# The linear memory's denominators in one bank, its main part divided one token tile at a time

## What is computed

```python
q = x @ Wq.T; k = x @ Wk.T; v = x @ Wv.T          # x normalised; 512, 128 and 128 columns
qh = q.reshape(b, s, N_QUERY, N_HEAD, D_HEAD)     # 4 x 8 heads of 16 columns
scores = jnp.einsum('bsqhd,bthd->bqhst', qh, kh) * scale
probs = jax.nn.softmax(scores, axis=-1)
a_dot = jnp.einsum('bqhst,bthd->bsqhd', probs, vh)
sigma_q = jax.nn.elu(q.reshape(b, s, N_QUERY, D_KV))
a_mem = sigma_q @ memory / (sigma_q @ memory_norm)   # memory 128 x 128, memory_norm 128 x 1
w = jax.nn.sigmoid(memory_weight)
out = a_dot * (1.0 - w) + a_mem * w
```

## Time and profile before

| | us |
|---|---|
| median of three runs (5053.01 to 5055.21) | 5054.02 |
| the profiled execution | 5102.55 |
| its span, first to last instruction | 5100.8 |
| PE busy in the span | 4587.9 (90%) |
| DVE busy | 3619.3 (71%) |
| ACT busy | 2408.7 (47%) |
| POOL busy | 716.7 (14%) |

### The profile page before, as it was taken

One profiled execution on the slowest core, in us unless ns is written; L12 is line 12 of the kernel. 1 busy time (PEld: TensorE's weight loads), 2 busy tenths in 40 slices (PEclk: granted clock), 3 DMA queues, 4 the chain that ended last, 5 costly groups with the idle time before them and its releaser, 6 DMA issues.

```text
span 5100.8 us, 144724 instructions
## 1 busy us (share of the span) xinstructions
PE 4587.9 (90%) x63104; PEld 3208.2 (63%) x63104; DVE 3619.3 (71%) x7890; ACT 2408.7 (47%) x4592; POOL 716.7 (14%) x909
## 2 busy tenths in 40 slices
PE   5799999999999998499999999999999999999988
PEld 4677777777777776456546646645654654665564
DVE  3666776666667666276787788778778778867876
ACT  3233433333333333164564565466456457546645
POOL 0000000000000000112211211221221221122121
PEclk9899999999999998699999999999999999999999
DMA  2222222222222222100000000000000000000000
GB/s 61 48 62 67 68 71 64 61 61 61 61 62 61 61 66 68 65 1 18 1 18 17 10 9 18 18 1 18 17 1 18 17 10 10 18 18 1 18 9 9
DMA packets 352134, 171.76 MB, mean 34 GB/s; under 512 B 300016, under 2 KB 300784, under 8 KB 350736
## 3 DMA queue, kind: packets, MB, share of 16 engines
q1 hardware_dynamic: 342528, 145.20, 10.7%
q10 hardware_dynamic: 8976, 17.30, 1.2%
HBM read 93.74 MB, written 67.63 MB: 32 GB/s over the span
## 4 chain that ended last, share of the span: by engine, by line
PE 43%; DVE 10%; ACT 3%; issue 1%; POOL 1%; DMA 1%; SPq 0%; DVEq 0%; ACTq 0%; POOLq 0%
PE row_psum L1698 9%; PE row_psum L1673 9%; PE row_psum L40 5%; DVE smax L1951 5%; PE row_psum L42 5%; PE row_psum L41 5%; PE row_psum L1686 4%; PE row_psum L1742 2%; ACT xr_hi L1325 1%; PE row_psum L1726 1%; PE row_psum L1463 1%; DVE probs L1931 1%; DVE stats L1785 1%; POOL rstd L1268 1%; PE row_psum L1645 1%
## 5 line engine op out<-in xcount | busy, mean ns | idle before, releaser
L1951 DVE TENSOR_REDUCE smax<-row_psum 128x1 f32<-128x512 f32 x2048 | 1269.3, 681 | 90.7 <-PE row_psum L1673 89.2
L1398 ACT ACTIVATE probs<-row_psum 128x512 f32<-128x512 f32 x2048 | 1092.6, 601 | 364.8 <-PE row_psum L1686 345.2
L1673 PE MATMUL row_psum<-k_stack,q_stack 64*128 64x512 f32 (+1 forms) x2048 | 738.0, 437 | 50.6 <-DVE smax L1951 24.5
L1686 PE MATMUL row_psum<-q_stack,k_stack 64*128 64x512 f32 (+1 forms) x2048 | 730.8, 457 | 20.8 <-ACT probs L1398 8.2
L1673 PEld LDWEIGHTS row_psum<-k_stack,q_stack 64*128 64x128 f32 (+1 forms) x2048 | 350.5, 186 | 504.0 <-DVE smax L1951 374.0
L1698 PE MATMUL row_psum<-probs,v_aug 128*32 128x512 f32 x4096 | 539.6, 604 | 1.7 <-ACT av_sb L1414 0.4
L1686 PEld LDWEIGHTS row_psum<-q_stack,k_stack 64*128 64x128 f32 (+1 forms) x2048 | 318.3, 184 | 220.2 <-ACT probs L1398 152.5
L868 DVE TENSOR_TENSOR lane_t<-lane_t,lane_p 128x30 f32<-128x30 f32 (+14 forms) x960 | 318.3, 332 | 33.0
L865 DVE TENSOR_TENSOR lane_p<-lane_t 128x30 f32<-128x30 f32 (+14 forms) x960 | 315.6, 329 | 23.5
L40 PE MATMUL span_bank<-x_hi,w_hi 128*128 128x256 f32 x1024 | 301.6, 295 | 33.6 <-DVE x_lo L841 33.0
L40 PE MATMUL row_psum<-wf_hi,xr_hi 128*128 128x320 f32 (+1 forms) x1024 | 331.1, 323 | 0.5 <-DVE xr_lo L1819 0.3
(11 more groups left out here) (209 smaller groups left out, 9883.8 us busy)
## 6 DMA issues: line engine op xcount, KB each, us to landing
x_sp<-in_x ACTq DMA_DIRECT2D x33, 512.0 KB, 4.1
tri_dram<-tri SPq DMA_DIRECT2D x256, 64.0 KB, 2.0
lane_t<-tri_dram SPq DMA_DIRECT2D x32, 512.0 KB, 4.7
inv_dram<-lane_t SPq DMA_DIRECT2D x32, 512.0 KB, 2.6
inv_b<-inv_dram SPq DMA_DIRECT2D x256, 64.0 KB, 2.3
x_res<-in_x SPq DMA_DIRECT2D x32, 512.0 KB, 3.9
x<-x_res SPq DMA_DIRECT2D x32, 512.0 KB, 3.8
xs<-x SPq DMA_DIRECT2D x16, 1024.0 KB, 5.5
```

The costliest lines, as they stand in the source:

```text
L1398: act.activation(probs[:, h % PROBS, tt, :], ps[:, m % STACK_BANKS, :], ACT.Exp, scale=float(DH) ** -0.5).then_inc(exp_ready, 1)
L1673: pe.matmul(ps[:, bank, :], q_stack[rows, qt, P * st:P * st + P], k_stack[rows, kv, :], start=True, stop=True).then_inc(max_mm, 1)
L1686: pe.matmul(ps[:, m % STACK_BANKS, :], k_stack[rows, kv, P * tt:P * tt + P], q_stack[rows, qt, :], start=True, stop=True).then_inc(score_m ...
L1951: dve.tensor_reduce(smax[:, g, st:st + 1], ps[:, bank_of("max", NT * g + st), :], AX.X, ALU.max).then_inc(max_ready, 1)
```

## The change

Each 129-column product is split. The denominators come first: `memory_norms(n)` multiplies, for group n, the four token tiles of `q_elu` with the norm column alone, four matmuls with one moving column each, into sixteen neighbouring columns of bank 7. It stands at four places of PE's loop (`NORM_SLOTS`): in both halves of step 3 and in the first halves of steps 4 and 5. DVE takes one reciprocal and one scaling of all sixteen in step 5. The main part keeps 128 columns; the four results of a token tile fill one bank, 6 or 7 in turn, and DVE multiplies them in one instruction of 512 columns. `MEM_LAG` is 6 in place of 5, so tiles 0 to 3 come in steps 6 to 9, and bank 7 joins the ring at step 10 in place of 9. Tile t waits for `amem_ready` of tile t-2 in place of t-1, and tile 1 for the reciprocals, which have to be out of bank 7. The first group of denominators also waits for the last `q_lo`, since bank 7 holds group 3 of q until DVE has taken that.

```diff
--- before.py
+++ after.py
@@ -1016,10 +1016,12 @@
 TURN_LAG = AV_LAG + 4
 OUT_LAG = TURN_LAG + 1
 MAXT_LAG = 4
-MEM_LAG = 5
+MEM_LAG = 6
+NORM_SLOTS = ((3, 0), (3, 1), (4, 0), (5, 0))
 STACK_BANKS = 3
 RING = (3, 4, 5)
 RING_LAST = 7
+MEM_BANKS = (6, 7)
 PROBS = 7
 NORM_STEP = NH + 1
 LEFT_STEPS = (NH + 3, NH + 5, NH + 6, NH + 11)
@@ -1133,7 +1135,7 @@
         k_mm = sem("row_k_mm"); khi_ready = sem("row_khi"); klo_ready = sem("row_klo"); v_mm = sem("row_v_mm"); vT_ready = sem("vT_ready")
         vtok_mm = sem("vtok_mm"); v_ready = sem("row_v_ready")
         ksel_mm = sem("ksel_mm"); keven_ready = sem("keven_ready"); kodd_ready = sem("kodd_ready"); qsel_mm = sem("qsel_mm"); qstack_ready = sem("qstack_ready")
-        mem_mm = sem("mem_mm"); amem_ready = sem("amem_ready"); amem_added = sem("amem_added")
+        mem_norm_mm = sem("mem_norm_mm"); mem_rc_ready = sem("mem_rc_ready"); mem_mm = sem("mem_mm"); amem_ready = sem("amem_ready"); amem_added = sem("amem_added")
         max_mm = sem("max_mm"); max_ready = sem("max_ready"); maxT_mm = sem("maxT_mm"); shift_ready = sem("shift_ready"); shift_in = sem("shift_in")
         score_mm = sem("score_mm"); exp_ready = sem("exp_ready"); av_mm = sem("av_mm"); av_ready = sem("av_ready")
         avT_mm = sem("avT_mm"); avn_ready = sem("avn_ready"); adot_added = sem("adot_added"); dve_own = sem("row_dve_own")
@@ -1633,17 +1635,25 @@
 
             def attention(b, following):
 
+                def memory_norms(n):
+
+                    pe.wait_ge(qelu_ready, at(b, NQ, n + 1))
+                    if n == 0:
+                        pe.wait_ge(qlo_ready, at(b, NQ, NQ))
+                    for t in range(NT):
+                        last = pe.matmul(ps[:, RING_LAST, NQ * t + n:NQ * t + n + 1], q_elu[:, n, P * t:P * t + P],
+                                         mem_aug[:, DKV:DKV + 1], start=True, stop=True)
+                    last.then_inc(mem_norm_mm, 1)
+
                 def memory(t):
 
-                    if t == 0:
-                        pe.wait_ge(qelu_ready, at(b, NQ, NQ))
-                        pe.wait_ge(qlo_ready, at(b, NQ, NQ))
-                    else:
-                        pe.wait_ge(amem_ready, at(b, NT, t))
+                    if t == 1:
+                        pe.wait_ge(mem_rc_ready, at(b, 1, 1))
+                    if t >= 2:
+                        pe.wait_ge(amem_ready, at(b, NT, t - 1))
                     for n in range(NQ):
-                        c0 = (DKV + 1) * (n % 2)
-                        last = pe.matmul(ps[:, 6 + n // 2, c0:c0 + DKV + 1], q_elu[:, n, P * t:P * t + P],
-                                         mem_aug[:, :], start=True, stop=True)
+                        last = pe.matmul(ps[:, MEM_BANKS[t % 2], DKV * n:DKV * n + DKV], q_elu[:, n, P * t:P * t + P],
+                                         mem_aug[:, 0:DKV], start=True, stop=True)
                     last.then_inc(mem_mm, 1)
 
                 def ring_bank(kind, n):
@@ -1732,6 +1742,8 @@
                             maximum(g, 2 * j + 1)
                         if g < NH and now:
                             score(*now[1])
+                        if (g, j) in NORM_SLOTS:
+                            memory_norms(NORM_SLOTS.index((g, j)))
                         if j == 0 and 0 <= g - MEM_LAG < NT:
                             memory(g - MEM_LAG)
                     quad, i = divmod(g - 3 - TURN_LAG, 4)
@@ -1919,19 +1931,21 @@
                 elu_exp(b, 2)
                 take_q_lo(1)
 
+                def memory_reciprocals():
+                    dve.wait_ge(mem_norm_mm, at(b, NQ, NQ))
+                    rc = mem_rc[:, :, :].rearrange("p t n -> p (t n)")
+                    mark(dve.reciprocal(rc, ps[:, RING_LAST, 0:NT * NQ]))
+                    dve.wait_ge(dve_own, own[0])
+                    dve.tensor_scalar(rc, rc, mem_w[:, 0:1], None, ALU.mult).then_inc(mem_rc_ready, 1)
+
                 def memory(t):
                     dve.wait_ge(mem_mm, at(b, NT, t + 1))
-                    pv = ps[:, 6:8, 0:2 * (DKV + 1)].rearrange("p c (n e) -> p c n e", n=2)
-                    rc = mem_rc[:, t, :].rearrange("p (c n) -> p c n", c=2)
-                    mark(dve.reciprocal(rc, pv[:, :, :, DKV]))
-                    dve.wait_ge(dve_own, own[0])
-                    mark(dve.tensor_scalar(rc, rc, mem_w[:, 0:1], None, ALU.mult))
-                    dve.wait_ge(dve_own, own[0])
-                    for c in range(2):
-                        last = dve.tensor_tensor(a_mem[:, t, 2 * DKV * c:2 * DKV * c + 2 * DKV].rearrange("p (n e) -> p n e", n=2),
-                                                 pv[:, c, :, 0:DKV],
-                                                 rc[:, c, :].rearrange("p (n o) -> p n o", o=1).to_broadcast([P, 2, DKV]), ALU.mult)
-                    last.then_inc(amem_ready, 1)
+                    if t == 0:
+                        dve.wait_ge(mem_rc_ready, at(b, 1, 1))
+                    dve.tensor_tensor(a_mem[:, t, :].rearrange("p (n e) -> p n e", n=NQ),
+                                      ps[:, MEM_BANKS[t % 2], :].rearrange("p (n e) -> p n e", n=NQ),
+                                      mem_rc[:, t, :].rearrange("p (n o) -> p n o", o=1).to_broadcast([P, NQ, DKV]),
+                                      ALU.mult).then_inc(amem_ready, 1)
 
                 for g in range(NH + OUT_LAG):
                     quad, i = divmod(g - 3 - OUT_LAG, 4)
@@ -1949,6 +1963,8 @@
                         if g < NH:
                             dve.wait_ge(max_mm, at(b, NT * NH, NT * g + st + 1))
                             dve.tensor_reduce(smax[:, g, st:st + 1], ps[:, bank_of("max", NT * g + st), :], AX.X, ALU.max).then_inc(max_ready, 1)
+                        if (g, st) == (NORM_SLOTS[-1][0], 2):
+                            memory_reciprocals()
                         if st == 2 and 0 <= g - MEM_LAG < NT:
                             memory(g - MEM_LAG)
                     if g in (1, 2):
```

## The result

The changed kernel takes 5174.49 us (median of four runs, 5168.76 to 5182.03) against 5054.61 for the kernel before on the same chip (four runs, 5053.01 to 5063.09). The ratio is 1.0223, 95% interval 1.0197 to 1.0248: 2.2% slower, 119.9 us between the medians, where 5070 us had been forecast.

What follows compares the result with a forecast made beforehand. DVE looked like the bound in the memory stretch, PE afterwards. DVE's 1.74 us saving a batch was outweighed by PE's slots and waits: values about 1.0 us late, 16 us in 16 batches, on 5054.02: 5070 us (5060 to 5082).

Steps and rivals of the forecast that it cites:

- r14: DVE's reduction number 14, counted as 4 × step + tile; forecast to start 0.50 us late, at 82.53 instead of 82.03.
- DVE's saving: Memory tiles and reciprocals on DVE: four tiles save 2.20 us, new reciprocal and scaling cost 0.46, net 1.74 a batch.
- A slot's price: PE time of four one-column denominator matmuls, eight passes: 0.81 us plus 0.09 for the slower instruction behind, 0.90 in all.
- Rival 3: Weight loads hidden on PE, so a slot costs nothing: 16 - 38 = -22 us, 5032; chance 0.09.
- rival 4: Weight loads unhidden on PE, so a slot costs 1.5 us: +39 us, 5109; chance 0.09.
- Steps 3 to 5 and the `q_lo` wait: PE becomes the bound: first slot waits for the fourth q_lo, DVE idles between reductions, reduction 22 starts 1.79 us late.
- Step 9: Bank 7 joins the ring later, so DVE gets a new idle of 0.79 us before reduction 38.
- the chain: Reduction 32, transposes, matmuls, exp, then ACT's shift ending at 100.5, for which maximum product 37 must wait.
- Rival 1: No stall at step 9: shift in time or product 38 clear of it; -2 us, 5052; chance 0.22.
- Who takes it on: From step 11 PE is the bound; values start about 1.0 us late in each batch, 16 us in 16.
- The clock: TensorE's granted clock, read as 1.00 (2.4 GHz) in the stretch; a reading below 1.00 would show the forecast wrong.
- Rival 2: DVE alone counts and PE's waits absorb the slots: -28 us, 5026; chance 0.10.

## Where the prediction held and where it failed

At full clock the working can be read against the changed kernel's own fourth batch. Times are from that batch's first reduction; the reductions are numbered as in the prediction.

| | before | forecast | full clock | third batch |
|---|---|---|---|---|
| r14 | 9.91 | 10.41 | 10.47 | 11.32 |
| r16 | 11.11 | 12.23 | 12.29 | 14.73 |
| r18 | 12.30 | 14.05 | 14.11 | 18.14 |
| r22 | 15.48 | 17.27 | 17.31 | 22.08 |
| r26 | 19.74 | 20.64 | 20.65 | 25.43 |
| r39 | 31.03 | 31.68 | 31.79 | 36.58 |
| first values | 32.85 | 33.85 | 34.19 | 38.98 |

- **DVE's saving.** Right. The division 0.681 us long with the next instruction 0.60 behind it, reciprocal and scaling of sixteen 0.43 for 0.46.
- **A slot's price.** Right at full clock: 0.81 us from its start to the next, 1.81 a half step for 1.82, taken from the durations of loads of other products. The experiment with 125 columns agrees that the loads and not the columns set it. Rival 3 (hidden loads, 0 us) and rival 4 (unhidden, 1.5 us) both fell.
- **Steps 3 to 5 and the `q_lo` wait.** Right at full clock: r22 1.83 late for 1.79; idle 0.48 in front of r14 for 0.50, and 0.52 to 0.56 in front of r16, r18 and r22 for 0.62.
- **Step 9.** Right, idle 0.83 in front of r38 for 0.79, released by the maximum product behind memory tile 3; ahead of that tile PE waits 0.67 us for ACT's shift, as the chain had it. It is there in every variant that keeps the order, without slots too (0.82). Rival 1 needed it gone.
- **Who takes it on.** The values are 1.3 us late for 1.0. Of the 0.3, 0.1 is there at r39 and the most of the rest between the last division's end and exp 12 (0.69 us for 0.53). From its first reduction to the next batch's the fourth batch takes 183.1 us for 182.0. ("PE 98% busy from there" is 99.5% in rows 2 and holds for those 11 us; in the 56 us behind them it is 96%, 53.76 busy.)
- **The clock.** This is the step that failed. The prediction read the clock of the stretch as 1.00 in the windows of the kernel before and priced every PE instruction at it. It named a clock below 1.00 as what would prove it wrong, but gave it no rival, no price and no chance. The change puts the slots into those same windows, and with them PE streams the same picks and maximum products over 1.81 us instead of 1.20. The clock fell in 14 of 16 batches, a half step went from 1.81 to 3.42 us, and the term that stood at zero was about 86 us of the profiled execution's 107.1.

Rival 2 (DVE alone counts) fell at the first slot, as DVE was idle in front of r14 at full clock too. The whole miss is 104 us (5174.49 for 5070). The full-clock terms account for about 5 (0.3 in each of 16 batches) and the clock in the token layers for about 86; the medians differ by 13 us more than the profiled token layers do, and no profile here says where those are. That the change came out slower, as forecast at 0.55, is mostly luck: the forecast's own mechanism gives 21 us of the loss.

**What the runs settle and what not.** Settled: the slots together with their `q_lo` wait bring the fall, as without both there is none; their columns matter, as 125 instead of one take it away in 14 of 16 batches with the wait, and in all 15 that had it without the wait, at no cost. The wait for `q_lo` is not needed, as 15 batches fall without it. Argued, not shown: that two waits close to each other are enough by themselves, from falls that begin 0.01 to 0.26 us after the first slot's start. Open: why two batches of sixteen escape with the same instructions (what differs between the batches of a profile is only when they start, and no run varied that), and whether the single slot of step 5 is harmless for want of the wait or because of its place. Not tried: the wait for `q_lo` in step 3 without any slot; slots with no wait of PE ahead of them at all; the denominators in a stretch in which PE streams densely, behind step 11.

## What to carry over

Before narrow matmuls with full weight loads go onto PE, price them twice, at both levels of the clock, together with all PE work beside them, and give the lower level a chance of its own; PE's busy share won't tell, since it read 100% at either. Where a narrow product's load sets its time anyway, its columns are free (up to 125 here), so merge it into a wide product, as the 129th column of the kernel before was, or widen it. And when a prediction names a reading that would refute it, that reading is a rival and needs a price.

## What was not expected of the hardware

- The granted clock fell from 1.00 to 0.50 behind idle times of PE of only 0.60 and 0.79 us, and stayed there while PE was busy without a gap (8.00 of 8.00 us). The Trainium skill (TensorE: Matmul & The Clock Gate, HAM oscillation — how this bites in real kernels) puts the falls in one kernel down to PE standing idle for some 3 to 5 us, for a DMA, between its groups of matmuls. These traces don't agree with that as the only way: no such long idle time is there, and what the matmuls are like counts too: behind the same 0.79 us 14 of 16 batches keep the clock with 125 columns and two do with one, and behind 0.94 us of the ring all sixteen keep it with 125 and one does with one.
- Adding columns made the kernel faster: 1.0223 with one column, 1.0066 with 125, in the same instructions at the same places (1.0180 with 32, within noise of one).
- At full clock a matmul with a 128x128 load takes the same time with one moving column and with 125: 0.10 us a pass, 54 instructions in the same 8 us.
- The delta rule layer, the same code in every kernel here, is between 2165 and 2204 us long, with 280 to 369 us at half clock, the least in the shortest and the most in the longest. A difference of 0.8% in the total of one execution can come from there.
